# Graph network on one core: POOL holds every fourth row gather until the chunk's earlier ones have landed

## The chip, the core and the metric

The kernel runs on one NeuronCore of one Trainium2 chip. The metric is the device time of the whole program in microseconds (us). TensorE is called PE, VectorE DVE, ScalarE ACT, GpSimd POOL and SyncE SP. A DMA is issued by one of these engines (SP, ACT or POOL here) and carried out by the core's 16 DMA engines.

## The reference

A graph network with N = 3125 nodes, 103,125 edges sorted by destination, 64 features and 4 layers. Each layer does this (`h` is the node table, `e` the encoded edge attributes, `t` one number per layer):

```python
msg = relu(h[src] + e) + 1e-7
m = msg * t
ex = exp(m - segment_max(m, dst)[dst])
alpha = ex / (segment_sum(ex, dst)[dst] + 1e-16)
out = h + segment_sum(msg * alpha, dst)
return relu(layernorm(out @ w1 + b1)) @ w2 + b2
```

Layers 1 to 3 take a normed and rectified `h` and add the result to `h`. A last layer norm over `x + ...` gives the output of 3125 x 64.

## The kernel before

The sorted edges are cut into two halves of 51,712 columns (padding included), one half on partitions 0 to 63 and the other on 64 to 127, features along the partitions. A layer runs over 54 chunks of columns (`NCH`): 49 of 1024 columns, then 512, 512, 256, 128 and 128. Every chunk goes through PE, ACT and DVE in this order:

- PE multiplies the edge attributes by the encoder weights into a PSUM tile `X` (`edge_product`, line 520) and adds `h[src]` to it. There are two ways to add `h[src]`. For a gathered tile, the rows are fetched from the table `z_table` in DRAM and turned by a PE transpose that accumulates in `X` (`add_rows`, line 547). For 23 chosen chunks (the even ones from 4 to 48), half of the columns is instead added by 150 matmuls against 0/1 matrices in fp8 (`add_by_one_hot`, line 537); those matrices are built by DVE in layer 0, kept in DRAM, and loaded again by DMAs of ACT's queue in layers 1 to 3 (line 696).
- ACT computes the message (line 647), its product with `t` (649) and, after DVE, the exponentials (659 to 664).
- DVE runs the segment maximum and the two segment sums as scans (885, 900, 916). SP stores the transposed sums to `rows_table` (347), four DMAs of 256 KB for a chunk of 1024.

After the last chunk the two halves are joined (lines 604 to 1039), POOL gathers the segments' ends (`agg`, line 494), and the node part computes the new `z_table`. The next layer starts when that is stored.

**The row gathers.** POOL issues them, one indirect DMA for each 128 edges of one half (line 479): 128 rows of 256 bytes, 32 KB. A full chunk of 1024 columns takes 16 gathers, a chosen one 8, the five narrow chunks 8, 8, 4, 2 and 2; the first chunk of a layer takes 14, since its first tile is padding. That is 622 per layer and 2488 in all. A chunk's gathers go to one of three buffers `gath[s]` (`SLOTS = 3`), and each adds 16 to the semaphore `gathered[s]` when it has landed. Before a chunk's first gather POOL waits for `x_ready`, which PE raises when it has turned the chunk that used the same buffer, three chunks earlier. PE waits for `gathered[s]` before it turns a chunk (line 545), for the count `GATHERS_UP_TO[g]`: the gathers into that buffer up to and with chunk `g`. The `agg` gathers (100) and, in layer 0, 25 gathers of sort keys (`gather_keys`, line 461, one after each of chunks 1 to 25) stand in the same POOL queue.

PE's order within a layer: transposes of chunk c, edge product of c+2, the last 90 one-hot matmuls of c+1 if c+1 is chosen, the first 60 of c+2 if that is chosen. The code is unrolled; each engine's instructions run in the order written, with waits on semaphores between.

Of the kernel before, what the change touches and what calls it, by code (L numbers as in the profile page):

```python
# [12 lines left out]
HALVES = 2  # L13
CH = 1024
KT = CH // P
BANK = 512
SLOTS = 3
XS = 4
SQ = 32
NSQ = CH // SQ  # L20
# [51 lines left out]
def first_tile(c):  # L72
    return SKIP if c == 0 else 0
# [19 lines left out]
def gathered_tiles(layer, c):  # L93
    return tiles(c) if one_hot_bank(layer, c) is None else BANK // P
# [14 lines left out]
GATHERS_UP_TO = []  # L109
for _g in range(LAYERS * NCH):  # L110
    _c = _g % NCH
    GATHERS_UP_TO.append((GATHERS_UP_TO[_g - SLOTS] if _g >= SLOTS else 0) + HALVES * (gathered_tiles(_g // NCH, _c) - first_tile(_c)))

assert sum(WIDTHS) == COLS and NCH % SLOTS == 0 and NCH % 2 == 0 and NT % GB == 0 and SUB * P == NB1H * BANK_COLS
assert all(tiles(c) == KT and c >= 3 for c in CHOSEN)


def gnn_kernel(nc, x_nodes, x_t, dst_stream, src_tiles, src_banks, attr_t, enc_node_w, enc_node_b, enc_edge_w, enc_edge_b,
# [12 lines left out]
    with ExitStack() as ctx:  # L131
# [37 lines left out]
        idx = sb("idx", [P, NBLK * KT * HALVES], i32)  # L169
        attr = slots("attr", SLOTS, [P, CH])  # L170
        gath = slots("gath", SLOTS, [P, KT * HALVES * F])
        msg = slots("msg", SLOTS, [P, CH])
# [109 lines left out]
        attr_landed, gathered, stored = sems("attr_landed", SLOTS), sems("gathered", SLOTS), sems("stored", 2)  # L282
# [157 lines left out]
        @block.gpsimd  # L440
        def _(pool):
            nc.gpsimd.memset(ident[:, :], 0.0).then_inc(ident_set, 1)
            pool.wait_ge(ident_set, 1)
            nc.gpsimd.affine_select(out=ident[:, :], in_=ident[:, :], compare_op=ALU.not_equal, fill=1.0, base=0,
                                    pattern=[[-1, P]], channel_multiplier=1).then_inc(ident_set, 1)
            nc.gpsimd.iota(node_i[:, :], pattern=[[P, NT]], base=0, channel_multiplier=1).then_inc(pool_set, 1)
            nc.gpsimd.memset(gath[0][:, 0:SKIP * HALVES * F], 0.0).then_inc(pool_set, 1)
            pool.wait_ge(pool_set, 2)
            pool.wait_ge(ident_set, 2)

            def settle():
                pool.sem_inc(settled, 1)

            def gather_keys(i):
                if i == 0:
                    pool.wait_ge(rows_found, 1)
                    pool.wait_ge(keys_stored, 16)
                if i >= KEY_SLOTS:
                    pool.wait_ge(keys_counted, i - KEY_SLOTS + 1)
                settle()  # L460
                pool.indirect_dma_start(out=key_rows[i % KEY_SLOTS], out_offset=None, in_=keys_dram,
                                        in_offset=bass.IndirectOffsetOnAxis(ap=row_i[:, i:i + 1], axis=0))\
                    .then_inc(keys_gathered[i % KEY_SLOTS], 16)

            for layer in range(LAYERS):
                if layer == 0:
                    pool.wait_ge(idx_landed, 16)
                    pool.wait_ge(z_stored, 16 * len(H0_GROUPS))
                else:
                    pool.wait_ge(z_stored, 16 * (len(H0_GROUPS) + layer * NG))  # L470
                for c in range(NCH):
                    g = layer * NCH + c
                    s = g % SLOTS
                    if g >= SLOTS:
                        pool.wait_ge(x_ready, g - SLOTS + 1)
                    settle()
                    for n in range(first_tile(c) * HALVES, gathered_tiles(layer, c) * HALVES):
                        col = STARTS[c] // P * HALVES + n
                        pool.indirect_dma_start(out=gath[s][:, n * F:(n + 1) * F], out_offset=None, in_=z_table,  # L479
                                                in_offset=bass.IndirectOffsetOnAxis(ap=idx[:, col:col + 1], axis=0))\  # L480
                            .then_inc(gathered[s], 16)
                    if layer == 0 and c in PREP_CHUNKS:
                        gather_keys(c - PREP_CHUNKS[0])

                pool.wait_ge(stored[0], 16 * NSTORE * ((layer + 1) * NCH // 2 + ((layer + 1) * NCH) % 2))
                pool.wait_ge(stored[1], 16 * NSTORE * ((layer + 1) * NCH // 2))
                pool.wait_ge(ends_stored, 16 * (layer + 1))
                if layer == 0:
                    pool.wait_ge(zero_stored, 16)
                    pool.wait_ge(pos_ready, 1)  # L490
                settle()
                for i, (t0, n) in enumerate(GROUPS):
                    for t in range(t0, t0 + n):
                        pool.indirect_dma_start(out=agg[:, t, :], out_offset=None, in_=rows_table,  # L494
                                                in_offset=bass.IndirectOffsetOnAxis(ap=pos_i[:, t:t + 1], axis=0))\
                            .then_inc(agg_gathered[i], 16)
# [708 lines left out]
```

## Time and profile before

| | |
|---|---|
| time, median of 3 runs | 4429.86 us (4423.26 to 4434.78) |
| span of the profiled execution | 4412.7 us |
| median less that span | 17.2 us |
| PE busy | 2914.6 us (66%) |
| DVE busy | 2824.3 us (64%) |
| POOL busy | 2517.9 us (57%) |
| ACT busy | 1741.2 us (39%) |

The profiled execution has no separate time of its own beside its span; the span runs from its first to its last instruction and is 17.2 us below the median of the runs, so what lies around it is taken as 17.2 us. Busy times are sums over one execution. No engine is near 100%, so the shares alone don't say which wait ends last; that has to be read from the stages: the four layers, and within a layer the regular part of chunk pairs.

### The profile page before, as it was taken

Reading aid. Unit: us, or ns where it says so; the run is one execution under the profiler, and the core shown is the slowest. Engines: PE = TensorE matmul, PEld = TensorE weight load, DVE = VectorE, ACT = ScalarE, POOL = GpSimd, SP = SyncE. Lnnn points to the kernel's source line nnn. Section 1 sums busy time; section 2 is a strip of 40 time slices with the busy share of each in tenths; the row PEclk is TensorE's granted clock in tenths of the full one; section 3 lists DMA queues with packets and bytes.
Section 4 is the critical chain, followed back from the end, with each engine's and each line's share of the span. In section 5 each row is a group of like instructions: output and inputs, shape, how many; then the busy total and the mean of one; then the engine's idle time right before and its main releaser. Section 6 shows DMA issues by size and latency. Waiting matters only on the chain.

```text
span 4412.7 us, 44760 instructions
## 1 busy us (share of the span) xinstructions
PE 2914.6 (66%) x16648; PEld 1382.9 (31%) x16648; DVE 2824.3 (64%) x2795; ACT 1741.2 (39%) x2192; POOL 2517.9 (57%) x2621
## 2 busy tenths in 40 slices
PE   3667677775437776777435777777742777777764
PEld 2223233332313333333222333333331333333333
DVE  6467678778436665666753666665763565666675
ACT  3356555545223333333432333333432333433343
POOL 6565656564366665666445666665627565655642
PEclk6778788877568888888656888887855787888875
DMA  6677778877237777777534777777734677777761
GB/s 153 162 219 204 215 195 222 219 198 174 59 100 204 204 204 192 204 204 204 133 81 115 204 204 204 205 205 201 191 76 104 160 199 199 204 202 190 211 153 40
DMA packets 1041338, 774.25 MB, mean 175 GB/s; under 512 B 914394, under 2 KB 935391, under 8 KB 1017504
## 3 DMA queue, kind: packets, MB, share of 16 engines
q1 hardware_dynamic: 934256, 446.17, 42.9%
q10 hardware_dynamic: 22048, 226.63, 14.0%
q0 software_dynamic: 84816, 98.59, 9.9%
q8 instruction: 131, 2.15, 0.2%
q14 instruction: 87, 0.71, 0.0%
HBM read 478.68 MB, written 292.44 MB: 175 GB/s over the span
## 4 chain that ended last, share of the span: by engine, by line
PE 41%; issue 23%; DVE 11%; ACT 10%; another core or an unknown queue 10%; POOL 4%; DMA 1%; SPq 0%; ACTq 0%; POOLq 0%; DVEq 0%
PE X L537 32%; PE X L520 5%; POOL gath L479 4%; DVE decay L885 3%; PE X L547 2%; DVE state_all L916 2%; ACT msg L647 2%; DVE X L890 1%; ACT shared L676 1%; ACT X L649 1%; ACT decay L659 1%; ACT X L664 1%; DVE state_all L900 1%; ACT decay L637 1%
## 5 line engine op out<-in xcount | busy, mean ns | idle before, releaser
L479 POOL DMA_INDIRECT gath<-z_table,idx x2488 | 2396.0, 963 | 1606.0 <-issue 750.5
L537 PE MATMUL X<-one_hot,z_parts 128*64 128x512 fp8e5 x13800 | 2103.0, 427 | 840.8 <-issue 773.1
L537 PEld LDWEIGHTS X<-one_hot,z_parts 128*64 128x64 bf16 x13800 | 939.4, 120 | 2071.2 <-issue 1542.8
L883 DVE TENSOR_TENSOR decay<-decay,top 128x1 f32<-128x1 f32 x216 | 34.2, 158 | 1358.5 <-ACT X L649 1179.6
L647 ACT ACTIVATE msg<-X,edge_bias 128x1024 f32<-128x1024 f32 (+2 forms) x216 | 228.2, 1057 | 1622.5 <-remote 1080.3
L520 PE MATMUL X<-attr,enc_edge 128*128 128x512 f32 x824 | 469.3, 688 | 221.9 <-issue 115.8
L659 ACT ACTIVATE decay<-X 128x1024 f32<-128x1024 f32 (+2 forms) x216 | 209.3, 969 | 791.7 <-DVE X L890 556.1
L871 DVE STREAM_TRANSPOSE rows_all<-state_all 128x1024 f32<-128x1024 f32 (+3 forms) x432 | 505.9, 1171 | 7.5
L885 DVE TENSOR_TENSOR_SCAN decay<-X,decay 128x1023 f32<-128x1023 f32 (+2 forms) x216 | 477.2, 2209 | 7.7
L900 DVE TENSOR_TENSOR_SCAN state_all<-decay,state_all,X 128x1024 f32<-128x1024 f32 (+2 forms) x216 | 468.2, 2167 | 20.0 <-ACT X L664 16.0
L916 DVE TENSOR_TENSOR_SCAN state_all<-decay,state_all,X 128x1024 f32<-128x1024 f32 (+2 forms) x216 | 468.0, 2167 | 0.0
L547 PE MATMUL X<-ident,gath 128*128 128x128 f32 x1248 | 206.3, 299 | 230.0 <-DMA gath<-z_table,idx 187.4
L520 PEld LDWEIGHTS X<-attr,enc_edge 128*128 128x128 f32 x824 | 157.7, 213 | 375.6 <-issue 366.1
L903 DVE SCALAR_TENSOR_TENSOR X<-msg,X 128x1024 f32<-128x1024 f32 (+2 forms) x216 | 250.5, 1160 | 7.5
L547 PEld LDWEIGHTS X<-ident,gath 128*128 128x128 f32 x1248 | 148.0, 150 | 340.4 <-DMA gath<-z_table,idx 200.8
L890 DVE TENSOR_TENSOR X<-X,decay 128x1024 f32<-128x1024 f32 (+2 forms) x216 | 250.0, 1157 | 0.0
L649 ACT ACTIVATE X<-msg,tcol 128x1024 f32<-128x1024 f32 (+2 forms) x216 | 229.5, 1062 | 7.2
L637 ACT ACTIVATE decay<-keep 128x1024 f32<-128x1024 uint8 (+2 forms) x216 | 212.8, 985 | 16.3 <-DMA keep<-keep_dram 16.3
L662 ACT ACTIVATE decay<-decay 128x1024 f32<-128x1024 f32 (+2 forms) x216 | 213.2, 987 | 0.0
L660 ACT ACTIVATE X<-X 128x1024 f32<-128x1024 f32 (+2 forms) x216 | 208.0, 963 | 0.0
L664 ACT ACTIVATE X<-X 128x1024 f32<-128x1024 f32 (+2 forms) x216 | 207.1, 959 | 0.0
L494 POOL DMA_INDIRECT agg<-rows_table,pos_i x100 | 95.1, 951 | 159.7 <-DMA rows_table<-ends_row 94.7
(155 smaller groups left out, 1182.3 us busy)
## 6 DMA issues: line engine op xcount, KB each, us to landing
rows_table<-rows_all SPq DMA_DIRECT2D x784, 256.0 KB
one_hot<-one_hot_dram ACTq DMA_DIRECT2D x69, 1920.0 KB
attr<-attr_t SPq DMA_DIRECT2D x196, 512.0 KB
one_hot<-one_hot_dram ACTq DMA_DIRECT2D x69, 1280.0 KB
one_hot_dram<-one_hot SPq DMA_DIRECT2D x23, 1920.0 KB
gath<-z_table,idx POOLq DMA_INDIRECT x2488
one_hot_dram<-one_hot SPq DMA_DIRECT2D x23, 1280.0 KB
keep<-keep_dram SPq DMA_DIRECT2D x192, 128.0 KB
```

The costliest lines, as they stand in the source:

```text
L479: pool.indirect_dma_start(out=gath[s][:, n * F:(n + 1) * F], out_offset=None, in_=z_table, in_offset=bass.IndirectOffsetOnAxis(ap=idx[:, c ...
L520: last = nc.tensor.matmul(X[g % XS][:, b:b + BANK], enc_edge2[:, :], attr[s][:, b:b + BANK], start=True, stop=False)
L537: last = nc.tensor.matmul(x[h * F:(h + 1) * F, BANK:CH], z_parts[:, i * GB + k, third, :], one_hot[:, i, k, h * BANK:(h + 1) * BANK], star ...
L547: last = nc.tensor.matmul(X[g % XS][:, k * P:(k + 1) * P], gath[s][:, k * P:(k + 1) * P], ident[:, :], is_transpose=True, start=False, sto ...
L637: nc.scalar.activation(decay[s][:, 0:w], keep8[k % KEEP_SLOTS][:, at:at + w], ACT.Copy, scale=BIG, bias=-BIG).then_inc(pen_ready, 1)
L647: nc.scalar.activation(msg[s][:, 0:w], X[g % XS][:, 0:w], ACT.Relu, bias=edge_bias[:, :]).then_inc(msg_ready, 1)
L649: nc.scalar.activation(X[g % XS][:, 0:w], msg[s][:, 0:w], ACT.Copy, scale=tcol[:, layer:layer + 1])\
L871: v.transpose(rows[g % 2][:, 0:w // SQ, q, :], state[g % 2][:, q, 0:w].rearrange("p (b j) -> p b j", j=SQ))\
L885: v.tensor_tensor_scan(out=m[:, 1:w], data0=x[:, 0:w - 1], data1=m[:, 1:w], initial=m[:, 0:1], op0=ALU.max, op1=ALU.add).then_inc(run_max, 1)
L890: v.tensor_tensor(x, x, m, ALU.subtract).then_inc(shifted, 1)
L900: v.tensor_tensor_scan(out=state[g % 2][:, 0, 0:w], data0=decay[s][:, 0:w], data1=X[g % XS][:, 0:w], initial=state[(g - 1) % 2][:, 0, befo ...
L916: v.tensor_tensor_scan(out=state[g % 2][:, 1, 0:w], data0=decay[s][:, 0:w], data1=X[g % XS][:, 0:w], initial=state[(g - 1) % 2][:, 1, befo ...
```

## The change

POOL now waits inside a chunk. Before the gather with number n, if n is a multiple of 4 and is not the chunk's first, it waits until all gathers of this chunk issued so far have landed, that is until `gathered[s]` has reached 16 times the count of the chunks before in that buffer plus those of this chunk. Nothing else is changed: same gathers, same buffers, same order, same sizes.

```diff
@@ -15,6 +15,7 @@
 SLOTS = 3
+HOLD = 4
@@ -475,6 +476,9 @@
                     settle()
                     for n in range(first_tile(c) * HALVES, gathered_tiles(layer, c) * HALVES):
+                        if n % HOLD == 0 and n > first_tile(c) * HALVES:
+                            before = GATHERS_UP_TO[g - SLOTS] if g >= SLOTS else 0
+                            pool.wait_ge(gathered[s], 16 * (before + n - first_tile(c) * HALVES))
                         col = STARTS[c] // P * HALVES + n
                         pool.indirect_dma_start(out=gath[s][:, n * F:(n + 1) * F], out_offset=None, in_=z_table,
```

The agg gathers and the key gathers have no such wait.

## Rows read from the trace of the kernel before

**Rows 1.** The page, part 5: line, engine, operation, count | busy, mean ns | idle.

```profile
L479 POOL DMA_INDIRECT gath<-z_table,idx x2488 | 2396.0, 963 | 1606.0 <-issue 750.5
L537 PE MATMUL X<-one_hot,z_parts 128*64 128x512 fp8e5 x13800 | 2103.0, 427 | 840.8 <-issue 773.1
```

**Rows 2.** POOL's timeline, regular part of layer 1: start, us, what [idle before].

```profile
1533.41 0.94 POOL L479 DMA_INDIRECT gath<-z_table,idx  x1 [0.31 <-issue]
1538.11 0.94 POOL L479 DMA_INDIRECT gath<-z_table,idx  x1 [3.76 <-remote]
1539.36 0.94 POOL L479 DMA_INDIRECT gath<-z_table,idx  x1 [0.30 <-issue]
...
1546.85 0.94 POOL L479 DMA_INDIRECT gath<-z_table,idx  x1 [0.31 <-issue]
1550.40 0.95 POOL L479 DMA_INDIRECT gath<-z_table,idx  x1 [2.61 <-remote]
...
1569.13 0.94 POOL L479 DMA_INDIRECT gath<-z_table,idx  x1 [0.30 <-issue]
1574.27 0.94 POOL L479 DMA_INDIRECT gath<-z_table,idx  x1 [4.20 <-remote]
```

**Rows 3.** Windows, layers 2, 1, 3 and 0 from first to last gather.

```profile
2253.00:3210.00 957.00, 661.35 (x3956) 302.82 (x3954) 590.90 (x446) 346.09 (x346) 589.48 (x622) 0.81 0.70 185
1188.00:2150.00 962.00, 666.29 (x3956) 306.03 (x3954) 590.55 (x446) 346.17 (x346) 589.16 (x622) 0.80 0.70 184
3313.00:4291.00 978.00, 673.31 (x3956) 308.53 (x3954) 590.10 (x445) 346.12 (x346) 589.24 (x622) 0.80 0.69 181
23.00:1082.00 1059.00, 703.00 (x3958) 310.97 (x3956) 771.12 (x619) 541.15 (x584) 652.37 (x647) 0.78 0.74 197
```

**Rows 4.** PE's timeline at layer 2's start: when chunks 0, 1 and 2 are turned.

```profile
2274.21 1.97 PE L547 MATMUL X<-ident,gath 128*128 128x128 f32 x8 [19.57 <-DMA gath<-z_table,idx]
2296.20 1.97 PE L547 MATMUL X<-ident,gath 128*128 128x128 f32 x8 [16.60 <-DMA gath<-z_table,idx]
2317.65 1.97 PE L547 MATMUL X<-ident,gath 128*128 128x128 f32 x8 [16.61 <-DMA gath<-z_table,idx]
```

**Rows 5.** POOL's timeline: the last gathers of those three chunks.

```profile
2271.82 0.94 POOL L479 DMA_INDIRECT gath<-z_table,idx  x1 [0.30 <-issue]
2291.79 2.17 POOL L479 DMA_INDIRECT gath<-z_table,idx  x1 [0.30 <-issue]
2312.99 0.94 POOL L479 DMA_INDIRECT gath<-z_table,idx  x1 [0.30 <-issue]
```

**Rows 6.** Windows around those landings (last three numbers: clock, DMA share, GB/s).

```profile
2271.00:2275.00 4.00, 0.79 (x4) 0.79 (x5) 0.00 (x0) 0.00 (x0) 3.09 (x4) 0.50 0.17 31
2291.00:2296.00 5.00, 0.00 (x0) 0.00 (x0) 2.15 (x2) 0.00 (x0) 4.08 (x4) 0.50 0.75 292
2313.00:2318.00 5.00, 0.35 (x2) 0.35 (x3) 0.00 (x0) 0.00 (x0) 3.78 (x5) 0.50 0.97 176
```

**Rows 7.** Chain of waits, end of layer 1: start, us, what.

```profile
2180.28 0.29 DVE ends_row L1039
2180.59 1.07 DMA rows_table<-ends_row
2181.79 0.73 issue
2182.52 0.94 POOL agg L494
```

**Rows 8.** POOL's timeline: last gather of layer 1.

```profile
2149.63 0.94 POOL L479 DMA_INDIRECT gath<-z_table,idx  x1 [0.30 <-issue]
```

**Rows 9.** PE's timeline in the regular part, one-hot matmuls of one chosen chunk.

```profile
1527.43 0.38 PE L537 MATMUL X<-one_hot,z_parts 128*64 128x512 fp8e5 x1 [0.18 <-issue]
1528.85 0.39 PE L537 MATMUL X<-one_hot,z_parts 128*64 128x512 fp8e5 x1 [1.04 <-issue]
...
1535.13 11.22 PE L537 MATMUL X<-one_hot,z_parts 128*64 128x512 fp8e5 x76 [1.52 <-issue]
```

**Rows 10.** Windows, L537 alone (PE, PEld, clock, DMA share, GB/s): layer 2's start, then regular.

```profile
2347.00:2365.00 18.00, 4.09 (x7) 0.77 (x6) 0.50 0.15 27
1514.00:1522.00 8.00, 6.67 (x60) 3.31 (x60) 1.00 1.01 308
```

**Rows 11.** Waits: POOL on a key's counting in layer 0, us in total, times, longest.

```profile
POOL agg L461 <- ACT junk L688: 58.0, 9, 6.7
```

## The prediction

> **What bounds the kernel now.** I started with the page's costliest groups. POOL's gathers are busy for 2396.0 us at 963 ns each, and the one-hot matmuls for 2103.0 us [rows 1]. Neither fills the span, so the question is whether POOL has time to spare inside a layer, and how much. POOL's timeline answers it. In the regular part of layers 1 to 3 it issues a gather every 1.25 us (0.94 of work, 0.30 between), 8 in a chosen chunk and 16 in a full one. After each chunk it stands idle for 2.6 to 4.2 us, until PE has turned the chunk three before [rows 2]. A pair of chunks thus repeats every 36.2 us (from 1538.11 to 1574.27), of which 24 x 1.25 = 30 us is issuing. POOL follows PE, but closely: its spare time is some 6 us in 36.
>
> The same holds over whole layers. Layers 1, 2 and 3 last 960.8, 955.4 and 977.3 us from first to last gather (the windows of [rows 3] are these bounds rounded outward), and 621 spacings of 1.25 us are 776 us. POOL's spare time is 185, 179 and 201 us per layer. Layer 0 lasts 1058.2 us with 647 issues, 646 x 1.25 = 808, so 250 us to spare, 58.0 of it waits for the counting of keys [rows 11].
>
> What holds PE back is, for a good part, not its own arithmetic. With 60 one-hot matmuls in 6.67 us at full clock it can run fast, yet at a layer's start it does 7 in 18 us with the DMA engines at 0.15, DVE and ACT idle and POOL issuing gathers all the time [rows 10]. In the regular part such single matmuls, 1.4 us apart, appear late in a full chunk's row of gathers (POOL's last one starts at 1533.41) and end shortly after it, at 1535.13 and on [rows 2, 9]. The releaser is "issue", so the trace names no cause. I keep this association for the rivals.
>
> **The change part by part.** It removes and moves nothing. It adds waits: at gathers 4, 8 and 12 of each of 26 full chunks of 1024 (78; the first chunk starts at number 2 and has three as well), at gather 4 of 23 chosen ones (23) and of the two chunks of 512 (2), none in the three last. That is 103 per layer, 412 in all.
>
> A wait costs POOL three terms. First the landing of the gather just issued, counted from its start; then the resumption after it; less the 1.25 us after which the next gather would have started anyway.
>
> The resumption: after the landing of the ends row POOL starts its next gather 0.73 us later, in the chain of waits [rows 7].
>
> The landing is not shown for gathers in the regular part, since nobody waits for them there. At a layer's start PE does. From the start of chunk 0's last gather to PE's transposes is 2274.21 - 2271.82 = 2.39 us; for chunks 1 and 2 it is 4.41 and 4.66 [rows 4, 5]. The first has the DMA engines at 0.17, the others at 0.75 and 0.97 [rows 6]. So the two ends are 2.39 (quiet) and some 4.5 (stores or loads beside it). A wait costs 2.39 + 0.73 - 1.25 = 1.87 us at the one and 3.98 at the other. A layer's DMA share is 0.70 now [rows 3] and falls if the layer grows, but it comes in full and in empty stretches. Half the waits at each end gives 3.4 us of landing. I take that, nearer the middle than the share alone says, because a wait also thins out the gathers that are under way together. The cost is then 3.4 + 0.73 - 1.25 = 2.88 us per wait and 297 us per layer.
>
> Behind a waiting POOL instruction stand only the gathers, the keys' gathers and, at a layer's end, agg's. Who waits for them is PE. A chunk pair has 4 waits: 30 + 4 x 2.88 = 41.5 us, against 36.2 now. POOL's spare time is used up, its lead of up to three buffers is used up within a few pairs, and then POOL sets the pace and PE waits for landings. Layers 1 to 3 become 776 + 297 = 1073 us from first to last gather: 112, 118 and 96 us more, together 326. Layer 0 becomes 808 + 297 = 1105, 47 us more; I take it that the waits for counted keys go, since ACT then has time.
>
> One term comes back. Today the last gather of layer 1 starts at 2149.63 and the ends row is ready at 2180.57, 31 us later [rows 7, 8], because POOL is well ahead of DVE there. When POOL is late, PE, ACT and DVE have little left when the last gather lands. The last six chunks after chunk 48's gathers hold 24 gathers and 2 waits, 36 us of POOL's time, in which DVE can do nearly all. I put what remains at 12 us, an estimate with bounds of 0 saved and 25 saved. That gives back 19 us per layer, 76 in all.
>
> The sum on the profiled execution: 4412.7 + 326 + 47 - 76 = 4710 us of span. With the 17.2 us around it that is 4727; I say 4730.
>
> The order of landing adds no cost of its own: the new wait counts the same semaphore that PE waits for. The wait before a chunk's first gather stays, but POOL, late, finds it already satisfied.
>
> **A rule weighed against the trace.** The rows show that a landing depends on the traffic: 2.39 us quiet, 4.41 and 4.66 beside other transfers [rows 4 to 6]. The Trainium skill, "DMA: Bandwidth & Descriptors", section "Anatomy of one DMA — SWDGE (gpsimd) path", gives about 2.0 us fixed, most of it the write receipt, plus bytes over 436 GB/s: an estimate of 2.08 us for 32 KB. By that a wait would cost 1.56 us and a layer 161, which POOL's spare time would hide. The quiet row agrees with the page within 0.3 us; the two loaded rows do not.
>
> **The rivals.**
>
> *The spare time hides it: no change.* Mechanism: all landings at 2.39 us or less, since gathers that wait for each other don't queue. Then the cost is 103 x 1.87 = 193 us per layer against 185, 179 and 201 of spare time, and the kernel stays at 4430 within 15 us. For it speaks that POOL idles before every chunk [rows 2]; against it the two loaded landings, in layers whose DMA share is 0.70 all along.
>
> *POOL's pauses free PE: faster.* Place: the one-hot matmuls that PE runs singly while POOL issues without a break [rows 9, 10]. If a pause of 2 us after four gathers is enough for PE to catch up, these stretches go, some 8 us per pair [rows 9] and at least the 18 us of [rows 10] at a layer's start. POOL is then the sole bound, with 969 us in layers 1 to 3 and 1001 in layer 0 at quiet landings: +14, -57, and the 76 us of the layers' ends come back too. That is 4430 + 14 - 57 - 76 = 4310. It decides only if the mean landing stays below about 2.7 us: above that POOL's own chain eats the gain. PE is probably freed in my forecast too; there it only means that PE waits for gathers instead.
>
> *Every landing is a loaded one: much slower.* At 3.98 us per wait a layer costs 410: 776 + 410 = 1186, so 225, 231 and 209 more, and 160 in layer 0; 4430 + 825 - 76 = 5180. It is what happens if POOL's stops fall together with the stores and loads that each chunk releases. The same side holds a case in which PE's single-matmul stretches last through POOL's short pauses and PE gets later as well.
>
> *The change does nothing.* The counts in the wait could be met early. They are the exact number of this buffer's gathers so far, so I give this nothing beyond the no-change case.
>
> **How the numbers follow.** Forecast 0.70, with its own range of 4530 to 4930 (landings of 2.9 to 3.9 us, each 0.1 us being 41 us). Every landing loaded, or PE later too: 0.16. Hidden: 0.06. Faster: 0.08. The range leaves out the no-change and faster cases and the far part of the loaded one: 4490 to 4990. A change of 0.3% is about what a measurement of this kernel can tell from none. Slower 0.86, same 0.06, faster 0.08.
>
> **What would show it.** In POOL's timeline, groups of four gathers with 2.9 us more between them than now (3.2 us of idle in all); the idle before a chunk's first gather down to some 0.4 us. PE waiting for DMA gath in most chunks and not at the layers' starts alone. A chunk pair of 41 us, layers of about 1070 us. The single one-hot matmuls of [rows 9] shorter or gone. The last gather of a layer nearer to its ends row. I am wrong on the size if the idle before gathers 4, 8 and 12 is not near 3.2 us on average, and wrong on the mechanism if POOL still waits for PE before chunks, or if PE waits for something other than gathers.

## The result, and the profile after

The changed kernel takes 4993.74 us (median of 4 runs, 4973.57 to 5009.53), the kernel before beside it 4432.32 us (4423.26 to 4436.77). The ratio is 1.126, with a 95% interval of 1.122 to 1.130: 561 us slower, where 300 were forecast. The profiled execution has a span of 4971.6 us and took 4973.57 us. Only 2.0 us lie around the span, and 1.8 to 2.1 in the other recorded executions; so the 17.2 us that the prediction adds must be mostly the distance of one execution from the median. The comparison of spans (559 us) and that of medians (561 us) agree.

First the page: two lines of its part 4 (shares of the chain that ended last, by engine and by line), then three of the costliest groups (busy, mean ns | idle before, releaser), which answer to [rows 1].

```profile
POOL 42%; issue 26%; DMA 23%; DVE 5%; ACT 1%; another core or an unknown queue 1%; PE 1%; SPq 1%; POOLq 0%; ACTq 0%; DVEq 0%
POOL gath L483 41%; DMA gath<-z_table,idx 22%; DVE shared L1063 1%; DVE decay L889 1%; POOL agg L462 0%; DVE zn L1094 0%; SPq L348 0%; DVE rows_all L875 0%; DVE sq L1083 0%; DVE state_all L920 0%; DVE state_all L904 0%; DVE X L894 0%; DVE shared L1052 0%; PE X L541 0%
...
L483 POOL DMA_INDIRECT gath<-z_table,idx x2488 | 2391.4, 961 | 2268.2 <-DMA gath<-z_table,idx 1486.7
L541 PE MATMUL X<-one_hot,z_parts 128*64 128x512 fp8e5 x13800 | 1705.7, 394 | 197.1 <-issue 192.9
L551 PE MATMUL X<-ident,gath 128*128 128x128 f32 x1248 | 284.6, 391 | 1853.0 <-DMA gath<-z_table,idx 1829.4
```

POOL's own instructions, the spacing between them ("issue") and the landings it waits for make up 91% of the chain: POOL sets the pace nearly throughout. Its busy time is what it was (2391.4 against 2396.0 us); new are 1486.7 us of idle before gathers, released by other gathers. PE now waits for landings before its transposes (1829.4 us). And the single one-hot matmuls of [rows 9] are mostly gone: "issue" before them went from 773.1 to 192.9 us. Both kernels do the same arithmetic and move the same bytes, so the difference has to be in what waits for what.

POOL's timeline over one pair of chunks, the regular part of layer 1, against [rows 2] (start, us, what, idle before):

```profile
1702.30 0.94 POOL L483 DMA_INDIRECT gath<-z_table,idx  x1 [0.30 <-issue]
1710.47 0.94 POOL L483 DMA_INDIRECT gath<-z_table,idx  x1 [7.22 <-DMA gath<-z_table,idx]
...
1718.18 0.94 POOL L483 DMA_INDIRECT gath<-z_table,idx  x1 [3.04 <-DMA gath<-z_table,idx]
...
1723.17 0.94 POOL L483 DMA_INDIRECT gath<-z_table,idx  x1 [0.30 <-issue]
...
1729.61 0.94 POOL L483 DMA_INDIRECT gath<-z_table,idx  x1 [1.75 <-DMA gath<-z_table,idx]
...
1743.26 0.94 POOL L483 DMA_INDIRECT gath<-z_table,idx  x1 [3.96 <-DMA gath<-z_table,idx]
...
1754.46 0.94 POOL L483 DMA_INDIRECT gath<-z_table,idx  x1 [6.51 <-DMA gath<-z_table,idx]
...
1762.21 0.94 POOL L483 DMA_INDIRECT gath<-z_table,idx  x1 [3.07 <-DMA gath<-z_table,idx]
...
1770.95 0.94 POOL L483 DMA_INDIRECT gath<-z_table,idx  x1 [0.30 <-issue]
1773.68 0.94 POOL L483 DMA_INDIRECT gath<-z_table,idx  x1 [1.79 <-DMA gath<-z_table,idx]
```

The pair repeats every 44.0 us (1710.47 to 1754.46, or 1718.18 to 1762.21), against 36.2 before. The four stops are 3.04 us (before gather 12 of a full chunk), 1.75 (gather 4 of a chosen one), 3.96 and 6.51 (gathers 4 and 8 of the next full one), and a pair later they are nearly the same again (3.07, 1.79). The gather at 1723.17 is the first of the chosen chunk: 0.30 us of idle, no wait for PE any more. The stops have a fixed place in the cycle, and so has the traffic beside them. The windows of the same stretch show it (last three numbers: TensorE clock, DMA share, GB/s):

```profile
1702.00:1706.00 4.00, 4.00 (x34) 1.73 (x33) 2.51 (x3) 1.35 (x2) 0.94 (x1) 1.00 0.95 333
1706.00:1710.00 4.00, 3.40 (x32) 1.58 (x28) 4.00 (x4) 2.55 (x3) 0.00 (x0) 1.00 0.57 239
...
1742.00:1746.00 4.00, 4.00 (x25) 1.84 (x22) 0.00 (x0) 2.23 (x2) 2.13 (x3) 1.00 1.12 203
1746.00:1750.00 4.00, 4.00 (x40) 2.14 (x38) 3.90 (x5) 0.00 (x0) 1.64 (x2) 1.00 0.89 354
1750.00:1754.00 4.00, 2.01 (x20) 0.81 (x16) 3.97 (x3) 3.94 (x5) 0.00 (x0) 1.00 0.86 293
...
1770.00:1774.00 4.00, 4.00 (x8) 1.33 (x8) 1.29 (x2) 2.23 (x2) 1.90 (x3) 0.50 0.13 25
```

The stop before 1754.46 lies in a DMA share of 0.89 and 0.86 and costs 6.51 us; the one before 1773.68 lies at 0.13 and costs 1.79. The busy stretch runs from about 1738 to 1766. SP issues four stores of the sums from 1737.91 to 1741.95 and then a load of attributes, ACT a load of 0/1 matrices, and SP four more stores from 1754.65:

```profile
1743.14 0.33 ACTq L700 DMA_DIRECT2D one_hot<-one_hot_dram  x1
1754.65 6.51 SPq L348 DMA_DIRECT2D rows_table<-rows_all  x4
```

The share alone doesn't give the length of a stop: the one before 1762.21 lies at 0.95 as well and costs 3.07. By place, the stops of chunks 6 to 47 in layers 1 to 3 average 1.93 us in chosen chunks and 3.65, 6.46 and 3.27 us before gathers 4, 8 and 12 of full ones.

The waits of POOL in layers 1 to 3 (us in total, times, longest), and the windows of layers 0 to 3 from first to last gather, which answer to [rows 3]:

```profile
POOL gath L483 <- DMA gath<-z_table,idx: 1110.9, 307, 8.4
```

```profile
22.00:1219.00 1197.00, 615.47 (x3962) 303.74 (x3961) 785.24 (x634) 548.76 (x596) 651.18 (x647) 0.74 0.66 176
1313.00:2427.00 1114.00, 618.58 (x3960) 302.72 (x3959) 598.62 (x454) 349.94 (x353) 587.27 (x622) 0.77 0.62 160
2523.00:3634.00 1111.00, 610.73 (x3961) 305.11 (x3959) 598.16 (x452) 349.80 (x353) 587.13 (x621) 0.77 0.62 160
3730.00:4857.00 1127.00, 625.07 (x3960) 309.98 (x3959) 598.22 (x453) 349.94 (x353) 587.08 (x622) 0.76 0.61 158
```

1110.9 / 307 is 3.62 us of idle per stop, so a stop costs 3.62 - 0.30 = 3.32 us. A layer should then last 776 + 103 x 3.32 = 1118 us; unrounded, layers 1 to 3 last 1112.7, 1109.9 and 1126.2. Layer 0 lasts 1196.0. That is 593 us more than before over the four layers (138, 152, 154.5 and 149).

Last, the chain at the end of layer 1, which answers to [rows 7, 8] (start, us, what). The last gather starts at 2426.39.

```profile
2434.76 1.24 SPq L338
2436.04 3.34 DMA keep<-keep_dram
2439.42 0.19 issue
...
2450.05 0.29 DVE ends_row L1043
2450.36 1.06 DMA rows_table<-ends_row
2451.55 0.73 issue
2452.28 0.94 POOL agg L498
```

The ends row is ready 24.0 us after the last gather, against 30.9 before.

### The profile page after: what moved, and what is told of

Its sections match the earlier page's. It is cut to its first block, busy times and chain, and to the rows that moved or that the text cites. A ratio compares the mean times of both kernels' runs of the same rounds, so it can differ in the third digit from the quotient of the medians.

```text
span 4971.6 us, 44760 instructions
## 1 busy us (share of the span) xinstructions
PE 2673.7 (54%) x16648; PEld 1374.1 (28%) x16648; DVE 2825.7 (57%) x2795; ACT 1742.0 (35%) x2192; POOL 2511.5 (51%) x2621
## 4 chain that ended last, share of the span: by engine, by line
POOL 42%; issue 26%; DMA 23%; DVE 5%; ACT 1%; another core or an unknown queue 1%; PE 1%; SPq 1%; POOLq 0%; ACTq 0%; DVEq 0%
POOL gath L483 41%; DMA gath<-z_table,idx 22%; DVE shared L1063 1%; DVE decay L889 1%; POOL agg L462 0%; DVE zn L1094 0%; SPq L348 0%; DVE rows_all L875 0%; DVE sq L1083 0%; DVE state_all L920 0%; DVE state_all L904 0%; DVE X L894 0%; DVE shared L1052 0%; PE X L541 0%
## 5 line engine op out<-in xcount | busy, mean ns | idle before, releaser
L483 POOL DMA_INDIRECT gath<-z_table,idx x2488 | 2391.4, 961 | 2268.2 <-DMA gath<-z_table,idx 1486.7
L541 PE MATMUL X<-one_hot,z_parts 128*64 128x512 fp8e5 x13800 | 1705.7, 394 | 197.1 <-issue 192.9
L551 PE MATMUL X<-ident,gath 128*128 128x128 f32 x1248 | 284.6, 391 | 1853.0 <-DMA gath<-z_table,idx 1829.4
L541 PEld LDWEIGHTS X<-one_hot,z_parts 128*64 128x64 bf16 x13800 | 819.8, 113 | 1174.7 <-issue 578.7
L551 PEld LDWEIGHTS X<-ident,gath 128*128 128x128 f32 x1248 | 214.4, 202 | 1975.3 <-DMA gath<-z_table,idx 1901.7
L524 PE MATMUL X<-attr,enc_edge 128*128 128x512 f32 x824 | 560.2, 816 | 46.7 <-DVE state_all L920 30.7
L524 PEld LDWEIGHTS X<-attr,enc_edge 128*128 128x128 f32 x824 | 201.6, 272 | 208.1 <-issue 199.2
```

Source lines behind the costliest of these rows:

```text
L524: last = nc.tensor.matmul(X[g % XS][:, b:b + BANK], enc_edge2[:, :], attr[s][:, b:b + BANK], start=True, stop=False)
L541: last = nc.tensor.matmul(x[h * F:(h + 1) * F, BANK:CH], z_parts[:, i * GB + k, third, :], one_hot[:, i, k, h * BANK:(h + 1) * BANK], star ...
L551: last = nc.tensor.matmul(X[g % XS][:, k * P:(k + 1) * P], gath[s][:, k * P:(k + 1) * P], ident[:, :], is_transpose=True, start=False, sto ...
```

## The experiments

They were run in five jobs, and each kernel is compared with the kernel before in the same job. The same kernel before took 4430, 4432 and 4403 us in three of them and 3567 and 3569 us in the other two: there the single matmuls are absent from the traces and POOL's gathers set the pace. What brings that about the runs don't say. It isn't the chip alone, since the record gives chip 1 for the first job (4430 us) and for the second (3567 us); each result below names the time beside it, and only such pairs are compared.

**Fewer stops: every eighth gather only.** 26 stops per layer, before gather 8 of the full chunks.

```diff
-HOLD = 4
+HOLD = 8
```

> Stops only before gather 8 of full chunks and tail chunks never: 26 per layer, 104 in all, instead of 103 per layer. Theory A (POOL's chain of issues and landings is the bound, and a layer has about 188 us of POOL time to spare): 26 x 3.3 = 86 us per layer fit in, POOL waits for PE before chunks again, and the time is that of before, 4430 us within 20; if the pause in the middle of a full chunk also ends PE's single matmuls, it is faster, down to 4300. Theory B (every wait for a landing costs the program a fixed part, whatever POOL has to spare; the change cost 561 us over 412 waits, 1.36 us each): 104 x 1.36 = 141 us more than before, 4573 us.

Measured: 4756.16 beside 4430.13, ratio 1.074 (1.070 to 1.077). Both expectations missed. The stops are short, 191.0 / 101 = 1.9 us of idle each, 1.8 in layers 1 to 3 (waits of POOL and PE, us in total, times, longest):

```profile
PE X L541 <- issue: 1070.8, 953, 3.1
POOL gath L483 <- PE X L551: 951.5, 102, 13.5
POOL gath L483 <- DMA gath<-z_table,idx: 191.0, 101, 5.8
```

POOL again waits for PE, 951.5 us in all, so here POOL is not the bound; the spare time exists, as theory A says, and what it missed is PE. PE lost its time at the one-hot matmuls, 1070.8 us of "issue" against 773.1 in [rows 1]. Its timeline shows where. POOL issues a gather every 1.25 us from 1717.84 to 1736.58 in this stretch, 16 without a stop:

```profile
1730.85 0.58 PE L541 MATMUL X<-one_hot,z_parts 128*64 128x512 fp8e5 x1 [0.80 <-issue]
1732.99 0.58 PE L541 MATMUL X<-one_hot,z_parts 128*64 128x512 fp8e5 x1 [1.56 <-issue]
1735.78 0.58 PE L541 MATMUL X<-one_hot,z_parts 128*64 128x512 fp8e5 x1 [2.21 <-issue]
1738.58 0.59 PE L541 MATMUL X<-one_hot,z_parts 128*64 128x512 fp8e5 x1 [2.22 <-issue]
1739.98 2.62 PE L541 MATMUL X<-one_hot,z_parts 128*64 128x512 fp8e5 x9 [0.81 <-issue]
```

PE falls to one matmul in 2.8 us, and is back in a run of 9 soon after POOL's row of gathers ends. A stop of 1.8 us at this place doesn't free PE. Why PE got slower than before isn't shown; that POOL's rows now lie differently against PE's is only a guess. The side of my slower rival, PE later as well, exists; it is not what the change itself does.

**One stop of three left out** (before gather 8 of a full chunk).

```diff
-if n % HOLD == 0 and n > first_tile(c) * HALVES:
+if n % HOLD == 0 and n != 8 and n > first_tile(c) * HALVES:
```

> The change without the stop before gather 8 of full chunks, which in layers 1 to 3 has the longest mean idle (5.67 us against 3.43 before gather 4, 3.30 before gather 12 and 1.91 in chosen chunks). 104 stops fewer than the changed kernel. Theory A with the cost tied to the place: 78 x 5.4 + 26 x 3.3 = 507 us less, 4490 us. Theory A with the cost tied to the burst of other transfers, which POOL then meets at its next stop: only the mean is saved, 104 x 3.3 = 343 us, 4650 us. Theory B: 104 x 1.36 = 141 us less, 4852 us.

Measured: 4596.06 beside 4430.13, ratio 1.040 (1.035 to 1.046). It is 166 us above the kernel before, the change 561; that is 395 us for 104 stops, 3.8 us each. The remaining ones average 1022.4 / 298 = 3.43 us of idle. At 3.33 us apiece the 104 stops would give 346, at this place's own mean 507, so both sides of theory A missed and theory B's 4852 is far off. POOL's timeline (chunks 6 to 47, layers 1 to 3) shows why: with the 6.46 us before gather 8 gone, the next stops but one, in the chosen chunks, grow from 1.93 to 3.63 us, while those before gathers 4 and 12 go from 3.65 to 3.46 and from 3.27 to 2.86. Part of the burst is met further on.

**The stops as fixed pauses, no landing awaited.** At the same 412 places POOL fills a spare tile of 128 x 1024 three times, each fill awaited.

```diff
+for _ in range(3):
+    nc.gpsimd.memset(pause_tile[:, :], 0.0).then_inc(paused, 1)
+    pauses += 1
+    pool.wait_ge(paused, pauses)
-pool.wait_ge(gathered[s], 16 * (before + n - first_tile(c) * HALVES))
```

> The same 412 places, but POOL doesn't wait for landings there: it fills a private tile of 128 x 1024 three times, each time waiting for the fill. The fill's length is not known from a row; call the mean idle at a stop with it p. Theory A (only the length of POOL's stops matters, not that it waits for a DMA): each layer lasts 776 + 103 x (p - 0.3) us from first to last gather, and if p is near 3.6 us, the mean in the changed kernel, the time is within 1% of the changed kernel's 4994. Theory B (waiting for the DMA itself costs): clearly under 4994 at the same p, below 4700.

Measured: 4817.74 beside 4430.13, ratio 1.088 (1.084 to 1.091). One such pause in POOL's timeline:

```profile
1501.56 0.94 POOL L487 DMA_INDIRECT gath<-z_table,idx  x1 [0.30 <-issue]
1502.50 2.98 POOL L483 MEMSET pause_tile<- 128x1024 f32 x3
1505.75 0.95 POOL L487 DMA_INDIRECT gath<-z_table,idx  x1 [0.27 <-POOL pause_tile L483]
```

A pause is 3.25 us between two gathers, 2.95 more than the plain 0.30. Layers 1 to 3 last 1082.4, 1081.3 and 1082.6 us; 776 + 103 x 2.95 = 1080. PE's idle by "issue" is 193.6 us, as in the changed kernel (192.9). So, once POOL sets the pace, what counts is how long it stands still, and it counts one to one. The landing matters only through its length.

**The wait one group later:** before gather 8 of a full chunk POOL waits for gathers 0 to 3, before gather 12 for 4 to 7, so that the newest four may still be under way. That is 208 waits; chosen chunks have none. Each group of four has its own semaphore, and PE waits for up to four of them.

```diff
+if n % HOLD == 0 and n >= 2 * HOLD:
+    k = n // HOLD - 2
+    pool.wait_ge(gathered[s][k], 16 * GROUP_UP_TO[g][k])
```

> Stops before gathers 8 and 12 of full chunks only, and there POOL waits only for the groups of four up to the last but one (gathers 0 to 3, then 4 to 7); the newest four may be under way. For this each group of four has its own semaphore, and PE waits for up to four of them. Theory A: a gather waited for was issued 5 us earlier or more, so most stops cost nothing and the few landings of 6 to 8 us cost 1 to 3 us; that fits in POOL's spare time: 4430 us within 30. Theory B: 208 waits x 1.36 = 283 us, 4713 us.

Measured: 4444.05 beside 4430.13, ratio 1.003 (1.0015 to 1.0047). That is theory A's 4430 within 30. Only 8 of the 208 waits show in the trace at all, 10.1 us together: four spacings are 5 us, which covers most landings. The whole came out 14 us slower. A wait that is met early costs next to nothing; draining the row costs.

**A quarter of the stores, with the change and without it.** In layers 1 to 3 SP stores only a quarter of each full chunk's sums; the output leaves the rest out.

```diff
+if layer > 0 and width(c) == CH:
+    n //= 4
```

> The changed kernel, but in layers 1 to 3 SP stores only the first quarter of each full-width chunk's sums (64 KB instead of 256 KB in each of four DMAs); the output is wrong for it. Theory S (the long landings at POOL's stops come from these stores of small rows running beside the gathers): the mean idle at a stop in layers 1 to 3 falls from 3.6 us to about 2.3, a layer from 1113 to about 980 us from first to last gather, the program to about 4590 us. Rival H (the loads of the 0/1 matrices and attributes are the cause): the idle stays above 3.3 us and the time above 4900.

> The kernel before with the same cut of the stores in layers 1 to 3. Theory G (PE's slow single one-hot matmuls come from POOL issuing gathers without a break, whatever the DMA engines do): the single matmuls stay, 4430 us within 1%. Rival D (they come from full DMA engines): they shrink and the time falls below 4300 us.

Measured beside 3566.87: with the change 4606.09, ratio 1.291 (1.289 to 1.293); without it 3562.21, ratio 0.9988 (0.9978 to 0.9997). POOL's stops in layers 1 to 3 of the first (within 1300 to 4900 us):

```profile
POOL gath L485 <- DMA gath<-z_table,idx: 834.4, 308, 6.2
```

2.71 us per stop where the change has 3.62 and theory S expected 2.3; the time is near its 4590, against the rival's 4900. By place, the stop before gather 8 falls from 6.46 to 3.23 us and the one before gather 4 of a full chunk stays (3.65 and 3.54). The job differs too, so the verdict on traffic is left to the run with stores and loads cut, below. The second run decides nothing between theory G and rival D, which both reckoned with 4430 us and single matmuls, and there are none here. It shows that the stores cost hardly anything where the kernel before takes 3567 (4.7 us), and what that condition is like (group of the page, then a window of layer 1):

```profile
L539 PE MATMUL X<-one_hot,z_parts 128*64 128x512 fp8e5 x13800 | 1534.2, 381 | 20.5 <-DVE one_hot L981 20.4
```

```profile
960.00:1740.00 780.00, 569.48 (x3970) 289.84 (x3970) 598.14 (x479) 348.72 (x355) 582.58 (x615) 0.85 0.60 180
```

No idle by "issue" is listed before the one-hot matmuls, against 773.1 us in [rows 1], and the layer lasts 778.4 us from first to last gather: the 621 spacings of 1.25 us. Here POOL has nothing to spare, and 16 gathers in a row don't slow PE.

**One pause of three fills before gather 8 only, in both conditions.** The fills of the third experiment with `HOLD = 8`.

> The kernel before with one fixed pause of 3.25 us of idle (three fills of a private tile) before gather 8 of each full chunk, 26 per layer. The stop of 1.8 us at the same place gave 4756 us. Theory G with a threshold (PE catches up only in a break of POOL's issuing of some 3 us or more): PE's single matmuls shorten and the time is 4350 to 4440 us. Rival K (any stop there moves the chosen chunk's gathers onto PE's 90 one-hot matmuls and loses the break between chunks): as with the short stop, 4700 us or more.

> The kernel before with one fixed pause of 3.25 us of idle before gather 8 of each full chunk, as once before. Beside 3567 us: theory A gives 104 x 2.95 = 307 us more, 3870 us. Beside 4430 us: threshold theory G (PE catches up in a break of 3 us) 4350 to 4440 us; theory K (the break before the chosen chunk's gathers is lost and PE's 90 matmuls get slower) 4700 us or more.

Measured: 3866.83 beside 3566.87, ratio 1.085 (1.083 to 1.087); 4415.34 beside 4431.73, ratio 0.997 (0.995 to 0.999). The same 104 pauses cost 300 us where POOL has nothing to spare (104 x 2.95 = 307) and not even 0 us where it has (-16). This is the plainest proof of what the spare time is worth. Beside 4430 theory G's range holds and theory K's is off, but PE has barely gained. It also qualifies the first experiment: at the same places 1.8 us of stop cost 326 us and 3.25 us none. PE's idle by "issue" is 1070.8 us there and 752.7 here:

```profile
PE X L545 <- issue: 752.7, 772, 3.1
```

**The change, twice more.** The changed kernel itself, in two further jobs.

> The changed kernel itself, since the kernel before took 4430 us beside the first four experiments and 3567 us beside the next four (there PE had no single matmuls and POOL's gathers ran back to back, 778 us per layer). POOL's chain (621 x 1.25 us plus 103 stops of 3.6 - 0.3 us per layer) doesn't depend on that: theory A expects 4900 to 5000 us whatever the kernel before takes, so a ratio of 1.13 beside 4430 or of 1.38 beside 3567. Rival: the stops cost what they cost beyond PE's slowness, 561 us: 4130 us beside 3567.

> The changed kernel itself once more. Beside 4430 us: 4990 us, as twice before. Beside 3568 us: POOL has nothing to spare there (778 us per layer from first to last gather, 621 x 1.25 = 776), so the whole chain shows: theory A 3568 + 412 x 3.3 = 4930 us, less what the layers' ends give back, 4850 to 4950. Rival (the stops cost 561 us in both): 4130 us.

Measured: 4988.69 beside 4431.73, ratio 1.126 (1.120 to 1.132), and 4954.17 beside 4403.06, ratio 1.127 (1.118 to 1.135). The result repeats.

**Stores and loads cut, with the change.** As with a quarter of the stores above, and in layers 1 to 3 also a quarter of each edge-attribute load and a fifth of the 0/1 matrices; all that is computed from the missing parts is left out of the output.

```diff
+w = width(c) // 4 if g > NCH and width(c) == CH else width(c)
-act.dma_start(one_hot[:, a:b].bitcast(f32), ...
+act.dma_start(one_hot[:, a:b, 0:1].bitcast(f32), ...
```

> The changed kernel with the stores of layers 1 to 3 cut to a quarter, and the loads of attributes to a quarter and of the 0/1 matrices to a fifth as well; the output is wrong for it. With the stores alone cut the mean idle at a stop in layers 1 to 3 was 2.71 us against 3.61. Theory S+H (landings are long because of all other transfers together, the rest of it by these loads): mean idle at or below 2.0 us, a layer of 950 us, the program 4390 us. Rival (a stop costs 2.7 us anyway): 4600 us.

Measured: 4490.95 beside 4431.73, ratio 1.015 (1.011 to 1.019). In layers 1 to 3:

```profile
POOL gath L486 <- DMA gath<-z_table,idx: 550.4, 287, 4.2
```

1.92 us per stop, against 3.68 with the full traffic in the same job (1121.9 us in 305 stops of the second run of the change), and layers of 948.8, 947.0 and 944.8 us. The stops are now nearly the same at all four places, 1.78 to 2.05 us on average (chunks 6 to 47), the 6.46 us before gather 8 included. This shows the second half of the mechanism: what a landing takes beyond the quiet one is other transfers' doing. The stops and the layers are as expected. The program came out 100 us above the expected 4390, which doesn't follow from its own 950 us a layer: in the changed kernel of this job layers 1 to 3 last 1122 us, so three of 950 give 4989 - 3 x 172 = 4473.

**A pause of one fill at the 412 places.**

```diff
-for _ in range(3):
+for _ in range(1):
```

> The 412 places of the change with a fixed pause of one fill of the private tile, 1.29 us of idle by the three fills' 3.25. Theory A: POOL's chain of a layer is 776 + 103 x 0.98 = 877 us. Beside 3567 us, where POOL has nothing to spare: 412 x 0.98 = 404 us more, 3970 us. Beside 4430 us it fits into the spare 188 us per layer: 4430 us, unless PE is made slower by POOL's now unbroken row of short-spaced gathers (theory K), then 4600 to 4800 us.

Measured: 4272.20 (4256.54 to 4284.09) beside 4431.73, ratio 0.964 (0.959 to 0.968): faster than the kernel before and the changed one. Neither expectation had that. PE's idle and one of POOL's pauses, 1.24 us between gathers:

```profile
PE X L545 <- issue: 360.7, 604, 4.1
```

```profile
1511.52 0.94 POOL L487 DMA_INDIRECT gath<-z_table,idx  x1 [0.31 <-issue]
1512.46 0.97 POOL L483 MEMSET pause_tile<- 128x1024 f32 x1
1513.70 0.95 POOL L487 DMA_INDIRECT gath<-z_table,idx  x1 [0.27 <-issue]
```

The idle by "issue" has halved from 773.1 us, layers 1 to 3 last 938.6, 935.9 and 950.0, and POOL's chain, 776 + 103 x 0.94 = 873, still fits beneath them. Part 4 of the page says the same of the chain: PE has 41% of it in the kernel before and 10% here, with DVE the largest engine at 25%. So the faster rival's mechanism is supported; it needs stops below those that the change makes. That the gain is PE's, and not some other effect of the fills, is argued from these two, not shown alone.

**Fills of other sizes, where POOL has nothing to spare.** A fill of 128 x 128 before every gather but a chunk's first (0.49 instead of 0.30 us between gathers), and two fills of 128 x 1024 at the 412 places (2.25 us).

```diff
+if n > first_tile(c) * HALVES:
+    nc.gpsimd.memset(pause_tile[:, 0:128], 0.0).then_inc(paused, 1)
```

> The kernel before with a small fill (128 x 128) and a wait for it before every gather but a chunk's first, about 0.25 us each, 565 per layer, in all 141 us per layer; the pause of 1.24 us before every fourth gather gave 4272 us. Theory R (the mean rate of issuing slows PE): as good as that, 4250 to 4330 us. Theory B4 (PE catches up only in a break of a us or so): PE stays slow and POOL has less to spare, 4430 us or more.

> The 412 places with two fills, 2.25 us of idle each: POOL's chain is 776 + 103 x 1.95 = 977 us in layers 1 to 3 and 808 + 201 = 1009 in layer 0. Both theories: POOL sets the pace, program about 4430 - 10 (the chain against 964 and 1058, some 35 given back at the layers' ends): 4400 to 4450 us, slower than the single fill's 4272. Rival (longer breaks free PE further and the time falls again): below 4250.

Measured beside 3568.85: 4002.47, ratio 1.122 (1.120 to 1.124), and 4335.72, ratio 1.215 (1.213 to 1.217). Both expectations were meant for 4430, so neither theory R nor B4 is tested, nor the rival of the second. The first has 2488 - 216 = 2272 fills; at 0.19 us they give 432, measured 434. That agreement is partly luck, since the layers 1 to 3 last 898.4, 898.8 and 898.8 us where 776 + 568 x 0.19 is 884: the mean idle is 0.21 us longer and not 0.19, and the layers' ends give some back. The second has 412 x 1.95 = 803, measured 767; its layers 1 to 3 last 977.2, 977.2 and 977.1 us, and 776 + 103 x 1.95 is 977. The law "776 plus what POOL stands still" holds for the layers within 1% at 1.95, 2.95 and 3.32 us.

**Fewer gathers, without any stop.** In layers 1 to 3 a full chunk issues only 8 of its 16 gathers, or 2; what the missing rows would add is left out of the result.

```diff
+def gathers(layer, c):
+    n = gathered_tiles(layer, c)
+    return HALVES * n if layer == 0 or width(c) < CH else min(HALVES * n, 8)
```

> The kernel before, but in layers 1 to 3 a full chunk of 1024 columns fetches only its first 8 gathers of 16 and PE turns old rows for the rest; the output is wrong for it. PE, ACT and DVE do the same work. Theory G (POOL's unbroken issuing slows PE): with 8 in a row at most and long breaks the single matmuls go, a pair of chunks falls from 36.2 to about 28 us, the program to about 3900 us. Rival: PE is slow for another reason, POOL only happens to be busy then: 4300 us or more.

> The kernel before with only 8 of 16 gathers in the full chunks of layers 1 to 3, PE turns old rows for the rest; the output is wrong for it. It took 3164 us where the kernel before took 3567. Beside 4430 us: theory G (POOL's issuing slows PE) - PE's single matmuls nearly vanish in layers 1 to 3 (8 in a row had none), a pair of chunks takes some 28 us instead of 36.2: 3900 us. Rival (PE is slow by itself in this condition): above 4250 us.

> The same with 2 gathers in every chunk of 1024 columns of layers 1 to 3, so that POOL is idle most of the time; the output is wrong for it. Theory G: as fast as e18 or faster, 3700 to 3900 us, no single matmuls at all in layers 1 to 3. Rival: above 4250 us.

> The kernel before with 8 of 16 gathers in the full chunks of layers 1 to 3; the output is wrong for it. Beside 3568 us: 3170 us, as twice before. Beside 4430 us: theory G (POOL's issuing slows PE) 3900 us or less; rival (PE is slow by itself) above 4250 us.

Measured: with 8 gathers 3164.11 beside 3566.87 (ratio 0.888, 0.886 to 0.889) and 3174.29 beside 3568.85 (0.890, 0.888 to 0.891); with 2 gathers 3120.95 beside 3568.85 (0.875, 0.873 to 0.876). In those jobs half of the gathers is worth 395 to 403 us, and the rest little more. Beside 4403.06 the same kernel takes 3590.43 (0.816, 0.810 to 0.822): 813 us, beyond theory G's 3900. Only this run tests the two theories, whose numbers were meant for 4430 us. POOL was not the bound there, it idled before every chunk; so the gathers held somebody else back. Group of the page, and one line of PE's timeline:

```profile
L542 PE MATMUL X<-one_hot,z_parts 128*64 128x512 fp8e5 x13800 | 1803.4, 402 | 441.1 <-issue 371.3
```

```profile
1711.63 9.90 PE L542 MATMUL X<-one_hot,z_parts 128*64 128x512 fp8e5 x90
```

The same 13800 matmuls have 371.3 us of "issue" before them instead of 773.1, and the 90 matmuls of a chosen chunk run through in 9.90 us, where the kernel before had singles among them [rows 9]. Layer 0, which keeps all its gathers, serves as a comparison within the run: its idle is 205.0 us in the kernel before and 191.2 here, and it lasts 1051 us against 1058, while in layers 1 to 3 the idle falls from 568.1 to 180.1 us and a layer from some 960 to 692. With fewer gathers PE is faster at work that has nothing to do with them. This run takes away both their issue and their transfers. That it is the issue is supported by the run with one fill, which has every transfer, only spaced, and half of the idle too; it isn't shown apart, and no row names what the two engines share. Nor is POOL's issuing enough by itself: where the kernel before takes 3567 us the same rows of gathers leave PE alone.

## Why the prediction was wrong in size and right in direction

The direction, the new bound and the waiters were as forecast. The time, 4994 against 4730, is just above the range's upper end of 4990. By the prediction's own steps:

- **How many stops.** 412 predicted, 409 listed as waits. Right.
- **Landing, 3.4 us: the step that failed.** Over all layers a stop has 1486.7 / 409 = 3.63 us of idle. With the 0.94 us of the gather before it, and less the resumption below, a landing averages 3.63 + 0.94 - 0.26 = 4.31 us, where I had 3.4. I had mixed the quiet 2.39 and the loaded 4.5 half and half "because a wait also thins out the gathers that are under way together". No row said so, and two things were wrong with it. The upper end was not an end: landings in the chain take up to 9.10 us, one of them 7.91 (below). And the mixing took the stops as spread evenly over busy and empty stretches. When POOL sets the pace, PE, DVE and SP follow it, so the transfers stand at a fixed place against the stops, and in the pair shown one stop in four falls where the DMA share is low. With the traffic cut the idle shrinks to 1.92 us and is nearly the same at every place.
- **Resumption, 0.73 us.** The chain has a landing and the resumption after it in two rows:

```profile
1702.30 7.91 DMA gath<-z_table,idx
1710.21 0.26 issue
```

  It is 0.26 us. The 0.73 of [rows 7] is what POOL takes after the ends row. This error hid half of the first: the landing was 0.91 us too low and the resumption 0.47 too high, and a stop costs 3.33 us (3.63 - 0.30) instead of 2.88. 412 x 0.45 = 185 us, the largest term.
- **Spare time of layer 0.** I took 646 spacings of 1.25 us. POOL's instructions are longer there: 651.18 / 647 = 1.01 us in the window of layer 0 against 587.27 / 622 = 0.94 in layer 1, and [rows 3] shows the same (652.37 for 647). With 646 x 0.30 that is 845 and not 808 us, 37 more. It was readable and I overlooked it.
- **The layers' ends, 76 us given back.** Measured: 593 more within the layers and 559 more of span (4971.6 - 4412.7), so 34. I had put what remains after the last gather at 12 us; it is 24.0 in layer 1. The chain shows that it is DVE's work on the small last chunks and one load of 3.34 us (`keep`), which start late because SP issues the load behind four stores. 42 us. (Behind chunk 48 there are five chunks, not six; the 24 gathers and 2 waits are right.)
- **The balance.** 412 stops of 3.33 are 1372 us. POOL had 815 us to spare within the layers by my count, 778 with layer 0 corrected; 1372 - 778 = 594, and the windows give 593. Less 34 that is 559. The forecast had 297 (326 + 47 - 76). The error of 262 us is thus 185 + 37 + 42, within 2 us. This is a balance of spans, into which the 17.2 us don't enter.
- **PE.** "Singles shorter or gone" came true (773.1 to 192.9 us) and bought nothing, as said, since PE waits for landings instead. The chunk pair of 41 us came out at 44.0.

Of the rivals, "hidden" fell with the landings. "Every landing is a loaded one" was put at 5180 and has the truer mechanism in part, with most stops falling together with stores and loads; its mean landing of 4.5 us was nearly reached (4.31), though by a mix from 2.47 to 9.10. It had 3.98 us per stop; with the measured resumption that is 3.51, near the 3.33. "Pauses free PE" holds below the length of stop at which POOL's chain passes PE's: shown at 1.24 us (4272 beside 4432), and gone at 3.25 (4818).

**A rule against the measurement.** By the rows the quiet landing is 2.47 us (1770.95 to 1773.68, less 0.26), the mean 4.31 and the longest seen in the chain 9.10. The Trainium skill, "DMA: Bandwidth & Descriptors", section "Anatomy of one DMA — SWDGE (gpsimd) path", puts the fixed part at about 2.0 us, an estimate of 2.08 for 32 KB; the same page's section "Latency and other measured facts" adds that the access to HBM is short on average and takes 2 us at high load. The first is within 0.4 us of the quiet landing and half of the mean, so beside traffic the measured landings stand and not a constant. The second points the right way: landings get shorter when the traffic is cut. That it is the access to HBM that takes longer no run here shows.

What stays open: why the same kernel takes 4430 us in one job and 3567 in another, and which of the loads (attributes or 0/1 matrices) lengthens the landings that the stores don't. The change wasn't run in the second kind. By an estimate from its law, at the 2.71 to 3.62 us of idle seen, it would add all of 412 x 2.41 = 993 to 412 x 3.32 = 1368 us there, less what the layers' ends give back; the one with a quarter of its stores added 1039. Nor is it settled why a stop of 1.8 us before gather 8 costs 326 us and one of 3.25 us none. The fastest version beside 4430, with one fill per four gathers, should by the same law cost 412 x 0.94 = 387 us where POOL has nothing to spare; it wasn't run there.

## What to carry to other kernels

Price a wait on a transfer's landing by the landing that will stand beside it after the change, not by a mean over today's traffic: an engine that sets the pace drags the bursts along, and its stops keep meeting them. Waiting for the group before the last, instead of the last, still bounds how far the gathers run ahead and cost 0.3%. An engine that idles while it waits for another may be what slows that other one: halve its work, or space it, before calling the idle time spare. And put the kernel before beside every run: here it came in two speeds, and an expectation written for one says nothing in the other.

## What of the hardware was not expected

- A 32 KB gather lands 2.47 us after its start with the DMA share at 0.13, 7.91 us with it at 0.95 and 0.57 in the two windows of 4 us after it; the longest in the chain takes 9.10 us.
- In three of the five later jobs PE issues one-hot matmuls singly, 1.4 us apart in the kernel before and up to 2.8 with a stop at gather 8, while POOL issues 16 gathers in a row; when POOL issues 8, 90 run through in 9.90 us. In the other two jobs the effect was absent altogether, and the kernel before took 3567 us instead of 4430.
- A fixed pause of 1.24 us after every fourth gather made the kernel 3.6% faster beside 4432 us; a pause of 3.25 us at the same places made it 8.8% slower beside 4430.
- POOL goes on 0.26 us after the landing of its own gather, and 0.73 us after that of the ends row.
